# Key and value scaling moved from VectorE to ScalarE, and a table step divided over two rounds, in a graph network kernel

## What is computed

```python
def gine_conv(x, edge_index, w1, b1, w2, b2):
    src, dst = (edge_index[0], edge_index[1])
    msg = jax.nn.relu(x[src])
    agg = jax.ops.segment_sum(msg, dst, num_segments=x.shape[0])
    h = x + agg
    h = jax.nn.relu(h @ w1 + b1)
    return h @ w2 + b2
out = jax.nn.relu(gine_conv(x, edge_index, w11, b11, w12, b12))
out = gine_conv(out, edge_index, w21, b21, w22, b22)
...
k = _layer_norm(k, ln_k_g, ln_k_b)          # over 64 features of each of 4 heads
v = _layer_norm(v, ln_v_g, ln_v_b)
kv = jnp.einsum('bhsd,bhse->bhde', k, v) / S
...
x = x + _L0_gnn_ref(...) + _L0_mix_ref(...)
```

## Time and profile before

| what | value |
|---|---|
| median of three runs | 4508.43 us |
| profiled execution, its span | 4520.99 us, 4519.3 us |
| PE, DVE, ACT, POOL busy | 3230.3, 3020.6, 2114.3, 2731.8 us |
| their shares of the span | 71%, 67%, 47%, 60% |
| DVE adds of both convolutions (L1492) | 1664, 701.9 us busy, 414.7 us idle before |
| gathers of the first convolution (L1458) | 832, 790.1 us busy, 384.2 us idle before |

### The profile page before, as it was taken

The page is one execution under the profiler, slowest core; times in us unless marked ns, Lnnn a source line. Parts: engine busy times, 40 slices in busy tenths (PEclk is TensorE's granted clock), DMA queues, the critical chain, the costliest instruction groups (busy, mean ns, idle before and its releaser), DMA issues. The chain is left out here.

```text
span 4519.3 us, 62899 instructions
## 1 busy us (share of the span) xinstructions
PE 3230.3 (71%) x14543; PEld 2390.6 (53%) x14544; DVE 3020.6 (67%) x7441; ACT 2114.3 (47%) x4996; POOL 2731.8 (60%) x2846
## 2 busy tenths in 40 slices
PE   4367777777766667777776947777777774599993
PEld 1155555555544545555555935565655553466662
DVE  5677777777766777777776437777777777644444
ACT  0334444434433334444443437777777775632220
POOL 0177776667647776777774657777777771034441
PEclk6588888888887888888888968888898886599996
DMA  2434433333323333333332211111111122311115
GB/s 90 132 110 115 118 114 108 109 109 113 109 83 108 110 102 98 110 110 110 109 110 70 70 44 35 34 35 34 35 34 34 35 30 23 143 44 60 60 61 191
DMA packets 233964, 378.40 MB, mean 84 GB/s; under 512 B 72570, under 2 KB 157027, under 8 KB 233404
## 3 DMA queue, kind: packets, MB, share of 16 engines
q0 software_dynamic: 120320, 278.00, 23.9%
q1 hardware_dynamic: 106896, 90.66, 6.3%
q10 hardware_dynamic: 6444, 6.40, 0.4%
HBM read 318.43 MB, written 56.42 MB: 83 GB/s over the span
## 5 line engine op out<-in xcount | busy, mean ns | idle before, releaser
L1482 PE MATMUL conv_ps<-conv_msg,conv_S 128*128 128x256 f32 x3328 | 1071.4, 471 | 406.5 <-DVE ACC L1492 313.3
L1482 PEld LDWEIGHTS conv_ps<-conv_msg,conv_S 128*128 128x128 f32 x3328 | 736.7, 235 | 652.8 <-DVE ACC L1492 317.0
L1458 POOL DMA_INDIRECT conv_msg<-relu_xn_table,GI x832 | 790.1, 950 | 384.2 <-issue 248.6
L1458 POOL DMA_INDIRECT conv_msg<-conv_table,GI x832 | 796.3, 957 | 327.5 <-issue 249.3
L2326 POOL DMA_INDIRECT gat_msg<-attn_table,GI x832 | 827.0, 994 | 266.6 <-issue 253.4
L1492 DVE TENSOR_TENSOR ACC<-ACC,conv_ps 128x256 f32 x1664 | 701.9, 422 | 414.7 <-issue 246.2
L1467 ACT ACTIVATE conv_S<-iota_row,LOC 128x128 f32<-128x128 f32 x1664 | 507.4, 388 | 541.2 <-PE conv_ps L1482 531.9
L2383 PE MATMUL gat_ps<-gat_M,gat_S 128*128 128x260 f32 x1664 | 508.4, 459 | 101.7 <-DVE gat_M L2484 96.7
L2383 PEld LDWEIGHTS gat_ps<-gat_M,gat_S 128*128 128x128 f32 x1664 | 366.3, 229 | 182.9 <-DVE gat_M L2484 112.2
L2441 DVE TENSOR_TENSOR ACC<-ACC,gat_ps 128x260 f32 x832 | 350.0, 421 | 33.4 <-PE gat_ps L2383 9.6
L1513 ACT COPY conv_hs<-ACC 128x256 f32 x98 | 39.6, 404 | 593.6 <-DVE ACC L1492 593.6
(11 more groups left out here) (549 smaller groups left out, 5770.1 us busy)
## 6 DMA issues: line engine op xcount, KB each, us to landing
conv_msg<-relu_xn_table,GI POOLq DMA_INDIRECT x832, 2.8
conv_msg<-conv_table,GI POOLq DMA_INDIRECT x832, 2.8
gat_msg<-attn_table,GI POOLq DMA_INDIRECT x832, 2.5
combine_y<-answers SPq DMA_DIRECT2D x24, 512.0 KB
relu_xn_table<-begin_rx SPq DMA_DIRECT2D x49, 128.0 KB, 1.7
xnT<-begin_xt SPq DMA_DIRECT2D x49, 128.0 KB, 1.8
conv_kv_xt<-xnT SPq DMA_DIRECT2D x49, 128.0 KB
conv_table<-conv_a SPq DMA_DIRECT2D x49, 128.0 KB
```

Of the source, the lines that this page charges most:

```text
L1458: pool.indirect_dma_start(self.msg[:, h * RING + k, :], None, table, bass.IndirectOffsetOnAxis(ap=self.m.GI[:, t:t + 1], axis=0)).then_inc ...
L1482: self.nc.tensor.matmul(self.ps[k % self.NB][:, 0:D], self.S[:, r % 2, k, :], self.msg[:, r % self.DEEP * RING + k, :], start=True, stop=T ...
```

## The change

Two edits.

In `KeyValueSums`, `dve_norm` keeps the reciprocal alone and signals a new semaphore `inverted`. A new function `act_norm` on ScalarE waits for it, and multiplies the eight groups of 64 columns with eight ACTIVATEs (Copy, the scale read from one column of `conv_kv_s`): four for the keys, four for the values. It stands after `act_root` and before the one-hot matrices of the next round, and it signals `kn_made`. The wait for `kn_used` goes to ScalarE too.

In `RunTables`, the part of a wide step for one table becomes a function `dve_sums_past(v, i, k)` with a drain at its start. Step i does `past` and table `frm` (k = 0) in its odd round, and table `to` (k = 1) follows in the next even round, also between adds 5 and 6.

```diff
     def dve_norm(self, v, i):
         nc = self.nc
         v.wait_ge(self.rooted, i + 1)
+        nc.vector.reciprocal(self.s2[:, :], self.rt[:, :]).then_inc(self.inverted, 1)
+
+    def act_norm(self, act, i):
+        act.wait_ge(self.inverted, i + 1)
         if i >= 1:
-            v.wait_ge(self.kn_used, i)
-        nc.vector.reciprocal(self.s2[:, :], self.rt[:, :])
-        v.drain()
-        r = self.s2[:, :].unsqueeze(2).broadcast_to([P, 8, 64])
-        nc.vector.tensor_tensor(self.groups(self.kn[:, :]), self.groups(self.pkv[:, 0:D]), r[:, 0:4, :], ALU.mult)
-        for c in range(2):
-            last = nc.vector.tensor_tensor(self.groups(self.vn[:, c, 0:P]), self.groups(self.pkv[:, D + c * P:D + c * P + P]),
-                                           r[:, 4 + 2 * c:6 + 2 * c, :], ALU.mult)
+            act.wait_ge(self.kn_used, i)
+        for g in range(8):
+            to = self.kn[:, g * 64:g * 64 + 64] if g < 4 else self.vn[:, (g - 4) // 2, g % 2 * 64:g % 2 * 64 + 64]
+            last = self.nc.scalar.activation(to, self.pkv[:, g * 64:g * 64 + 64], ACT.Copy, scale=self.s2[:, g:g + 1])
         last.then_inc(self.kn_made, 1)
...
+    def dve_sums_past(self, v, i, k):
+        nc, t = self.nc, (self.frm, self.to)[k]
+        v.drain()
+        nc.vector.tensor_tensor(self.by[:, 0:TILES - 1], t[:, 1:TILES], t[:, 0:TILES - 1], ALU.subtract)
+        v.drain()
+        nc.vector.tensor_tensor(self.picked, self.past, self.by[:, 0:TILES - 1].unsqueeze(1).broadcast_to([GROUPS, RUNS // 8, TILES - 1]),
+                                ALU.mult)
+        v.drain()
+        nc.vector.tensor_reduce(self.at[k][:, RUNS // 8 * (i - 9):RUNS // 8 * (i - 8)], self.picked, X_AXIS, ALU.add)
+        v.drain()
...
-            for k, t in enumerate((self.frm, self.to)):
...
+            v.drain()
+            self.dve_sums_past(v, i, 0)
...
                 if here(i := turn_of(r, 3)):
                     kv.act_root(act, i)
+                    kv.act_norm(act, i)
...
                     tables.dve_step(v, k)
+                if here(k := turn_of(r, 2, 17)) and k >= 9:
+                    tables.dve_sums_past(v, k, 1)
```

More of the change, by code:

```diff
@@ L380, in __init__ @@
         self.pkv, self.sums = st.ps("pkv"), st.ps("kv")
-        (self.centred, self.xt_in, self.projected, self.squared, self.root_in, self.rooted, self.kn_made, self.kn_used,
-         self.sums_done) = (st.sem(n) for n in ("centred", "xt_in", "projected", "squared", "root_in", "rooted", "kn_made",
+        (self.centred, self.xt_in, self.projected, self.squared, self.root_in, self.rooted, self.inverted, self.kn_made, self.kn_used,
+         self.sums_done) = (st.sem(n) for n in ("centred", "xt_in", "projected", "squared", "root_in", "rooted", "inverted", "kn_made",
                                                 "kn_used", "sums_done"))
```

## The result

| | median | range, runs | against before on the same chip |
|---|---|---|---|
| before | 4511.25 us | 4506.62 to 4516.53, 4 | |
| changed | 4468.61 us | 4466.20 to 4473.91, 4 | ratio 0.9902 [0.989, 0.9914] |

The change makes the kernel 42.6 us faster. Forecast were 4470 us, a gain of 38.7 us; the measured time lies in the stated range. The kernel before has one run more here than above, which moved its median from 4508.43 to 4511.25 us. The profiled execution took 4473.91 us, its span 4472.2 us, against 4520.99 and 4519.3. These are the busy times after (us, share of the span, number of instructions); ScalarE's has grown by 75 us over the whole kernel and VectorE's has shrunk by 40.

A forecast was written before the change was run, and what follows sets the result against it. VectorE was taken to bound the first convolution, at 21.25 us a pair plus 0.45 us of slow PE. Saving 0.90 us x 43 = 38.7 us, with 0 from the second edit, gave 4508.4 - 38.7, about 4470 us; range 4452 to 4498 us.

The forecast's parts named there:

- VectorE is the loop: First convolution: VectorE sets a pair's length, 21.25 us plus 0.45 us of slow PE; removing multiplications saves 0.90 us.
- Copies of 1.78 us, the projection at plus 2.28: First convolution: eight ScalarE copies take 1.78 us; PE's projection starts 2.28 us after the reciprocal, 1.03 us later than before.
- Slack at add 4: First convolution, odd round: 0.3 us remain between PE's sum 4 and VectorE's add 4, where a hand-over needs 0.15.
- One-hot matrices 2.1 us to spare: ScalarE's one-hot matrices, queued behind the copies, end at reciprocal plus 5.8 us; PE needs them at plus 7.9.
- the last sign against the forecast: First convolution: a clock below 1.00 from the reciprocal to the rank product in many pairs would show the forecast wrong.
- GpSimd allows 54 us: First convolution: gathers need 20.0 us a pair, so up to about 54 us can go before they set the pace.
- Edit 2 between +1.6 and -2.5 us: Second convolution, dividing the wide step: costs 1.6 us over eight steps, may save 2.5 us of waiting; taken as 0.
- A: Rival: PE speeds up too, all 0.45 us of lateness a pair goes, 4454 us; chance of below 4457 us 0.12.
- B: Rival: clock falls more often (4504 us) or copies are long (4496 us); 4484 to 4500 us had chance 0.12.
- D: Rival: freed VectorE time becomes waiting for PE, 4508 us; chance 0.07 together with the upper end of B.
- C: Rival: longer gap puts PE's projection at half clock, 3.2 us per affected pair, up to 4607 us; chance 0.07.
- The sum: Whole kernel: 38.7 us saved, 4521.0 to 4482.3 us profiled; by the median 4508.4 - 38.7, about 4470 us.

The follow-up runs named there:

- e3: The kernel before without VectorE's three multiplications, nobody scaling keys and values: 4460.06 us, ratio 0.9891.
- e4: The kernel before with ScalarE's eight scaling copies added, VectorE still doing its three multiplications into spare tiles: 4514.19 us, ratio 1.0014 against before.
- e1: Only the scaling of keys and values moved to ScalarE, run tables as in the kernel before: 4461.95 us, ratio 0.9898 against before.
- e7: The changed kernel with ScalarE's eight copies made twice, first into a spare tile: 4578.82 us, ratio 1.0151 against before.
- e5: The changed kernel run again, nothing altered: 4469.37 us, ratio 0.9905 against before.
- e10: The kernel before with ScalarE's square put ahead of its relu and copy in the even round: 4489.16 us, ratio 0.9953 against before.
- e8: The changed kernel without squares and variances: 4461.26 us, ratio 0.9884 against before.

## Why the prediction was right

- *VectorE is the loop, and edit 1 takes 0.90 us a pair out of it.* Right, shown by e3 and e4: without the multiplications on VectorE the pair is 20.5 us, with them 21.75, wherever the scaling is done. 0.90 x 43 = 38.7 us was forecast. The loop gave 0.94 us, and 0.17 us less lateness came with it; 1.11 x 43 = 48 us in the profiled execution, 48.9 us by the stage's ends. The cause was forecast rightly; the term was sized 0.2 us a pair too small.
- *Copies of 1.78 us, the projection at plus 2.28.* 1.76 and 2.13 us. One copy is 0.33 us long and the next starts 0.20 us after it, where 0.31 and 0.21 were taken. The estimate of 2.0 us from the Trainium skill ("ScalarE: Activation LUTs", section "What ACT_TABLE_LOAD costs") was too long. The Trainium skill's advice to multiply on VectorE ("ScalarE: Activation LUTs", section "Rules for kernel authors") goes by the price of the one operation; here VectorE was the loop, and moving the multiplications to the engine that needs longer for them made the kernel 45 us faster (e1).
- *Slack at add 4, 0.3 us where 0.15 is needed.* Add 4 came without delay in all 43 pairs, though put down to PE in each. That wording was named as a sign against the forecast; the 0.20 us in front of it show that it cost nothing. e7 shows the other side: 1.6 us more copies put 1.3 us of waiting before it (1.49 less 0.20), even at full clock.
- *One-hot matrices 2.1 us to spare.* They start at plus 1.82 and end at plus 5.5 where 5.8 was forecast. PE's first sum of the next round came at plus 7.9. The clock from the reciprocal to the rank product was 1.00 in all 43 pairs, so the last sign against the forecast didn't show either.
- *GpSimd allows 54 us; its waits fall to about 15 us.* Off in size: they fell to 2.1 us, since the pair got shorter than forecast and 16 gathers take 20.3 us rather than 20.0. The last gather is at 1275.2 where 1268 was forecast, though the stage ended earlier, because the adds' lag shrank too, which I had not reckoned with.
- *Edit 2 between +1.6 and -2.5 us, taken as 0.* About +2 us, so just outside; the wide pairs took 24.56 us on average where 24.0 to 24.3 were named as the sign (24.26 in the kernel before, not the 24.14 of the earlier trace rows). The group of VectorE's adds, 1523 to 1718 us, with the subtractions:

```profile
L1498 DVE TENSOR_TENSOR ACC<-ACC,conv_ps 128x256 f32 x128 | 53.9, 421 | 29.1 <-issue 25.3 <-PE conv_ps L1488 3.8
...
L1340 DVE TENSOR_TENSOR conv_by<-conv_to 50x48 f32<-50x48 f32 x8 | 1.6, 200 | 1.1 <-issue 0.4
...
L1340 DVE TENSOR_TENSOR conv_by<-conv_frm 50x48 f32<-50x48 f32 x7 | 1.4, 200 | 0.9
```

  The adds' idle time rose from 28.1 us to 29.1, where I had allowed it to fall to 25.6: the waits put down to PE did fall from 8.9 to 3.8 us, but those put down to nothing rose from 19.1 to 25.3, so most of what had stood under PE's name was not lateness of PE and could not go. The subtraction for `frm` has 0.13 us in front of it and overlapped before.
- *A, all of PE's lateness goes.* A third of the lateness went (0.17 of 0.55 us). It went by the clock, as A had it, but not by the moved gap that A gave as the reason: e3 kept the gap and had the same. Nor was all of it PE's: about half of the 0.55 us lies in adds 4 to 7 of the even round, where half clock is shown. *B* and *D* didn't occur. B's price was read too low: the longest pair before is 22.66 us (from 616.36), not the 22.48 of the earlier trace rows. *C* didn't occur at a gap of 1.19 us; at 2.83 us it did, and 26 pairs of it cost 40 us, nearly all that edit 1 saves.
- *The sum.* 4521.0 - 38.7 was 4482.3 for the profiled execution, which took 4473.9. Of the medians of one chip, 42.6 and, repeated, 45.1 us came where 38.7 were forecast (e5: 4514.48 - 4469.37), and 45.2 and 48.2 us with edit 1 alone. The terms not foreseen are 0.2 us a pair more, 9 us, and 2 us lost in the second convolution: 45.7 us with them. The forecast of the gain was thus 4 to 6 us too small by the medians, and 8.4 us in the profiled executions.

## What to carry to other kernels

Find the engine that has work or bare hand-overs from end to end in one period, and price a move by what leaves that loop, not by busy shares: 0.90 us came out, though ScalarE needs about twice VectorE's time for the same product. Before loading another engine, count the slack to the next instruction that waits for it, and the gap that opens on TensorE; here 1.2 us was harmless and 2.8 us was not. A stage's mean clock doesn't price a pair: look at the clock over the few instructions that the loop waits for, pair by pair. A wait that you remove may have hidden something: e10 got half of its 1.05 us.

## What was new about the hardware

- A gap on TensorE of the same length, 2.83 us, left the clock at 2.4 GHz in 11 pairs of e7 and not in 26 others of the same trace (1.00 and 0.79 over the 8 us from the reciprocal on in the two shown). The clock ahead of the pair differed: 0.71 in the first shown and 0.87 in the second, over the 3 us before the reciprocal.
- TensorE's clock rose from 0.84 to 0.92 over the stage and its busy time fell by 65 us; what shortened the pair was only that half clock lay over four sums of the even round in 3 pairs instead of 11, at about 0.75 us each.
- Eight scaled copies of 128x64 out of PSUM on ScalarE follow one another 0.20 to 0.21 us apart and are 0.33 us long each; two of 72 and 4 columns were 0.22 apart.
- 16 indirect gathers of 128 rows took 20.3 us when they set the pace (e8), and a few in the changed kernel waited for landings (8.1 us in 7 waits).
